# Layer 2 of a graph network: where the one-hot of each edge's target node is compared, turned and scaled

## The reference, cut to what matters

```python
proj = feat @ fc_weight.T
el, er = proj[src], proj[dst]                       # one row per edge
e = sum(leaky_relu(el + er, 0.2) * a, axis=-1)
gate = sigmoid(sum(el * er, axis=-1))
w = sigmoid(e * gate)                               # one weight per edge
neigh_sum = segment_sum(feat[src] * w[:, None], dst)
out = layernorm(x + (1 + eps) * feat + neigh_sum / max(deg, 1))
```

## Time and profile before

| what | value |
|---|---|
| median of 3 runs (lowest to highest) | 4249.38 us (4241.9 to 4252.88) |
| the profiled execution, first to last instruction (span) | 4202.4 us |
| median of the runs less that span | 47.0 us |
| layer 2's loop, first and last er+el (L1529) | 1644.2 to 4153.9 us |
| GpSimd's gathers L1449, 1624 of them | 1543.0 us, 950 ns each |
| VectorE's weigh L1461, 1632 | 477.5 us, 359 ns each |
| ScalarE's two comparisons L1556 and L1559, 406 each | 714 and 722 ns each |
| ScalarE's weight L1564, 407 | 202 ns each |

### The profile page before, as it was taken

One profiled execution on the slowest core, in us unless ns is written; L12 is line 12 of the kernel. 1 busy time (PEld: TensorE's weight loads), 2 busy tenths in 40 slices (PEclk: granted clock), 3 DMA queues, 4 the chain that ended last, 5 costly groups with the idle time before them and its releaser, 6 DMA issues. The chain is left out here.

```text
span 4202.4 us, 64915 instructions
## 1 busy us (share of the span) xinstructions
PE 2278.9 (54%) x13842; PEld 1815.0 (43%) x13842; DVE 2546.9 (61%) x12793; ACT 1628.2 (39%) x3531; POOL 2103.2 (50%) x2223
## 2 busy tenths in 40 slices
PE   1757575756667783445544444454444444444444
PEld 1535353544445443444443443444444444444443
DVE  6535353534444275667666676666676767667667
ACT  2424242433333244444443443443444444434344
POOL 3252434343343203666656565666656666656652
PEclk9878787878878896666666666656666666656666
DMA  7121111111111215444444444444444445444443
GB/s 145 32 54 31 51 34 48 38 44 42 41 48 34 58 49 169 138 132 136 134 133 129 123 137 128 130 137 128 136 125 131 134 132 139 129 135 129 128 129 96
DMA packets 357885, 425.07 MB, mean 101 GB/s; under 512 B 174163, under 2 KB 242141, under 8 KB 357740
## 3 DMA queue, kind: packets, MB, share of 16 engines
q0 software_dynamic: 103728, 266.13, 22.4%
q1 hardware_dynamic: 251800, 156.64, 14.5%
q10 hardware_dynamic: 2212, 0.60, 0.1%
HBM read 399.44 MB, written 23.70 MB: 101 GB/s over the span
## 5 line engine op out<-in xcount | busy, mean ns | idle before, releaser
L1449 POOL DMA_INDIRECT got<-rows,idx x1624 | 1543.0, 950 | 1038.3 <-issue 487.4
L1618 PE MATMUL sum_ps<-whot,got 128*128 128x128 f32 x3264 | 762.0, 410 | 1146.7 <-remote 416.6
L1618 PEld LDWEIGHTS sum_ps<-whot,got 128*128 128x128 f32 x3264 | 660.8, 301 | 1236.9 <-remote 433.6
L763 POOL DMA_INDIRECT got<-x_rows,idx x532 | 516.5, 971 | 789.5 <-DMA idx<-src_rows 630.7
L918 ACT CAST work<-c_ps 128x318 bf16<-128x318 f32 x1092 | 451.3, 431 | 845.0 <-remote 439.6
L945 PE MATMUL span_ps<-x_parts,work 128*126 128x393 bf16 x2756 | 667.9, 353 | 20.0 <-issue 20.0
L1611 PE MATMUL er_ps<-win,hot_t 128*128 128x128 bf16 x4932 | 525.4, 284 | 204.4 <-issue 121.0
L994 PE MATMUL c_ps<-right,left 128*128 128x318 bf16 x1092 | 338.0, 317 | 467.9 <-issue 281.2
L1611 PEld LDWEIGHTS er_ps<-win,hot_t 128*128 128x128 bf16 x4932 | 476.9, 134 | 234.7 <-issue 131.6
L1461 DVE TENSOR_SCALAR whot<-iota_f,dl,w_s 128x128 f32<-128x128 f32 x1632 | 477.5, 359 | 124.1 <-issue 121.7
L1517 DVE CUSTOM_DVE_ANT_0 small_rows<-got,er_ps 128x128 f32<-128x128 f32 x1624 | 387.3, 281 | 154.6 <-issue 116.3
(11 more groups left out here) (240 smaller groups left out, 2101.7 us busy)
## 6 DMA issues: line engine op xcount, KB each, us to landing
work<-dst_row SPq DMA_DIRECT2D x413, 256.0 KB
got<-rows,idx POOLq DMA_INDIRECT x1624
win<-parts SPq DMA_DIRECT2D x118, 96.0 KB
got<-x_rows,idx POOLq DMA_INDIRECT x532
idx<-src_rows SPq DMA_DIRECT2D x413, 2.0 KB
parts<-split SPq DMA_DIRECT2D x13, 384.0 KB
x_rows<-x_parts SPq DMA_DIRECT2D x2, 2320.5 KB
rows<-nodes SPq DMA_DIRECT2D x13, 256.0 KB, 2.8
```

The source lines that it names most:

```text
L763: pool.indirect_dma_start(got[:, c, i, 0:3 * D], None, x_rows, bass.IndirectOffsetOnAxis(ap=idx[:, c, i:i + 1], axis=0)).then_inc(gathered ...
L1449: pool.indirect_dma_start(got[:, c, i, :], None, rows, bass.IndirectOffsetOnAxis(ap=idx1[:, c, i:i + 1], axis=0)).then_inc(gathered[c], 16)
L1618: mm = pe.matmul(sum_ps[:, 0:P], got[:, c, i, D:2 * D], whot[:, c, i, :], start=(c == 0 and i == 0), stop=(c == NS - 1 and i == STEP - 1))
```

## The change

The targets are stored as 16-bit integers (`dst_row`, `dst_b`). VectorE now makes `hot_t`, with one comparison for a chunk's 512 edges against the partition's node number (`node_no`), 5 chunks ahead. TensorE then turns `hot_t` back, with the identity as the second operand, into the chunk's own PSUM bank `er_ps`, once `larger` has read that bank for the last time. ScalarE copies it from there, scaled by the weights, into `whot`. The column-wise targets (`dl_in`, `first_dl`, `dl`) and their two DMAs per body go. TURN becomes 5 and EXPAND 4.

```diff
-EXPAND = 5
-TURN = 6
+EXPAND = 4
+TURN = 5
...
-    dst_row = nc.dram_tensor("dst_row", [1, NBT * P * P], F32).ap()
+    dst_row = nc.dram_tensor("dst_row", [1, NBT * P * P], I16).ap()
...
 SyncE
-                        sp.wait_ge(less_done, k + 1)
+                        sp.wait_ge(node_done, k + 1)
                         sp.sem_inc(body_begun, 1)
                         load_first(k + 1)
-                        col = column(sp, k)
-                        sp.wait_ge(dl_done, k + 1)
-                        sp.sem_inc(body_begun, 1)
-                        sp.dma_start(dl_in[:], dst_rows[:, bass.ds(col, GROUP)]).then_inc(body_in, 16)
-                        sp.dma_start(first_dl[:], first_row[:, bass.ds(k, 1)].to_broadcast([P, 1])).then_inc(body_in, 16)
...
-                            sp.wait_ge(apart_done, NS * k + c + 1)
+                            sp.wait_ge(hot_done, NS * k + c + 2)
...
 VectorE
-                    def weigh(c, n):
-                        dve.wait_ge(w_done, n + 3)
-                        for i in range(STEP):
-                            at = c * STEP + i
-                            m = dve.tensor_scalar(whot[:, c, i, :], iota_f[:], dl[:, at:at + 1], w_s[:, c, i:i + 1],
-                                                  ALU.is_equal, ALU.mult)
-                        m.then_inc(whot_done, 1)
+                    def match(c, k):
+                        m = NS * k + c
+                        dve.wait_ge(dst_in[c], 16 * k + 16)
+                        dve.wait_ge(node_done, k + 1)
+                        dve.wait_ge(turned_back, m - TURN + 1)
+                        dve.tensor_scalar(hot_t[:, c, :], dst_b[:, c, :], node_no[:], None, ALU.is_equal
+                                          ).then_inc(hot_done, 1)
+
+                    def number(k):
+                        dve.wait_ge(first_in, 16 * k + 16)
+                        dve.wait_ge(hot_done, NS * k + 1)
+                        dve.tensor_scalar(node_no[:], first_t[:], pos[:], None, ALU.add).then_inc(node_done, 1)
...
                             if c == LATE:
-                                dve.wait_ge(body_in, 48 * k + 48)
-                                dve.wait_ge(whot_done, n)
+                                dve.wait_ge(body_in, 16 * k + 16)
                                 dve.sem_inc(body_begun, 1)
                                 dve.reg_mov(now, dve.value_load(at_now[0:1, 0:1], min_val=0, max_val=N - 1))
-                                dve.tensor_scalar(dl[:], dl_in[:], first_dl[:], None, ALU.subtract
-                                                  ).then_inc(dl_done, 1)
+                                number(k + 1)
...
+                            match((c + TURN) % NS, k + (c + TURN) // NS)
                             score((c - 1) % NS, n - 1)
-                            if c == LATE:
-                                dve.wait_ge(dl_done, k + 2)
-                            dve.wait_ge(summed, n + 1)
-                            weigh((c - 2) % NS, n - 2)
                             gated((c - 1) % NS, n - 1)
...
 ScalarE
-                    def match(c, k):
...
-                        act.activation(apart1[:], dst_b[:, c, :], ACT.Abs, bias=less[:]).then_inc(apart_done, 1)
...
-                        act.activation(hot_t[:, c, :], apart1[:], ACT.Relu, scale=-1.0, bias=one1[:]
-                                       ).then_inc(hot_done, 1)
+                    def weigh(c, n):
+                        act.wait_ge(turned_back, n + 3)
+                        act.wait_ge(w_done, n + 2)
+                        act.wait_ge(summed, n + 2)
+                        for i in range(STEP):
+                            m = act.activation(whot[:, c, i, :], er_ps[:, c, i * P:(i + 1) * P], ACT.Copy,
+                                               scale=w_s[:, c, i:i + 1])
+                        m.then_inc(whot_done, 1)
...
-                            if c == 1:
-                                offset(k + 1)
-                            match((c + TURN) % NS, k + (c + TURN) // NS)
                             weight((c - 1) % NS, n - 1)
+                            weigh((c - 1) % NS, n - 1)
...
 TensorE
+                    def turn_back(c, n):
+                        pe.wait_ge(l_done, n + 3)
+                        for i in range(STEP):
+                            mm = pe.matmul(er_ps[:, c, i * P:(i + 1) * P], hot_t[:, c, i * P:(i + 1) * P], ident_b[:],
+                                           start=True, stop=True)
+                        mm.then_inc(turned_back, 1)
...
-                        pe.wait_ge(whot_done, n + 3)
+                        pe.wait_ge(whot_done, n + 4)
...
-                            pe.wait_ge(l_done, n + 1)
+                            pe.wait_ge(whot_done, n + 1)
                             expand((c + EXPAND) % NS, k + (c + EXPAND) // NS)
                             if c == LATE + 1:
                                 pe.wait_ge(added, k + 1)
                                 sum_rows(0, n - LATE - 1)
                             if c != LATE:
                                 sum_rows((c - LATE) % NS, n - LATE)
+                            turn_back((c - 1) % NS, n - 1)
```

More of the change, by code:

```diff
@@ L1353, in graph_layers @@
             win_in = [sem(f"win_in{h}") for h in range(2)]
[L1354 to L1355 removed]
+            node_done = sem("node_done")
+            turned_back = sem("turned_back")
             hot_done = sem("hot_done1")
@@ L1496, in _ @@
                     dve.memset(er_ps[:, NS - 1, :], 0.0).then_inc(zeros_set, 1)
[L1497 to L1498 removed]
+                    dve.memset(hot_t[:, NS - 1, :], 0.0).then_inc(zeros_set, 1)
+                    dve.tensor_tensor_reduce(pr_s[:, 0, :], ident[:], iota_f[:], 1.0, 0.0,
                                              ALU.mult, ALU.add, pos[:]).then_inc(zeros_set, 1)
[L1500 removed]
                     dve.wait_ge(zeros_set, 9)
[L1502 to L1503 removed]
+                    dve.sem_inc(hot_done, 1)
+                    number(0)
+                    for c in range(TURN):
+                        dve.wait_ge(dst_in[c], 16)
+                        dve.wait_ge(node_done, 1)
+                        dve.tensor_scalar(hot_t[:, c, :], dst_b[:, c, :], node_no[:], None, ALU.is_equal
+                                          ).then_inc(hot_done, 1)
                     dve.sem_inc(leaked, 1)
@@ L1542, in _ @@
                     score(NS - 1, last)
-                    weigh(NS - 2, last - 1)
                     gated(NS - 1, last)
-                    weigh(NS - 1, last)
                     add_body(dve.snap(before, min_val=0, max_val=N - 1), bodies)
@@ L1564, in weight @@
                         act.activation(w_s[:, c, :], eg_s[:, c, :], ACT.Sigmoid).then_inc(w_done, 1)
-                    def offset(k):
-                        act.wait_ge(first_in, 16 * k + 16)
-                        act.wait_ge(apart_done, NS * k)
-                        act.activation(less[:], first_t[:], ACT.Identity, scale=-1.0, bias=pos[:]).then_inc(less_done, 1)
-                    act.sem_inc(hot_done, 1)
-                    act.wait_ge(zeros_set, 9)
-                    act.wait_ge(first_in, 16)
-                    act.activation(less[:], first_t[:], ACT.Identity, scale=-1.0, bias=pos[:]).then_inc(less_done, 1)
-                    for c in range(TURN):
-                        act.wait_ge(dst_in[c], 16)
-                        act.wait_ge(less_done, 1)
-                        act.wait_ge(hot_done, c + 1)
-                        act.activation(apart1[:], dst_b[:, c, :], ACT.Abs, bias=less[:]).then_inc(apart_done, 1)
-                        act.wait_ge(apart_done, c + 1)
-                        act.activation(hot_t[:, c, :], apart1[:], ACT.Relu, scale=-1.0, bias=one1[:]
-                                       ).then_inc(hot_done, 1)
+                    def weigh(c, n):
[6 more added lines that the diff above has]
+                        m.then_inc(whot_done, 1)
+                    act.wait_ge(zeros_set, 9)
+                    act.sem_inc(whot_done, 2)
                     for q in range(NQ):
@@ L1623, in _ @@
                     pe.sem_inc(summed, NS - LATE)
+                    pe.sem_inc(turned_back, 1)
                     for c in range(EXPAND):
```

27 lines of the change are left out of this document (6 added, 21 removed).

## The result

| | before | after |
|---|---|---|
| median, runs of one chip | 4241.05 us (4224.44 to 4260.55) | 4262.32 us (4232.07 to 4272.06) |
| span of the profiled execution | 4202.4 us | 4243.5 us |

The ratio is 1.0035, 95% interval 1.0021 to 1.0048: slower by a third of a per cent, where 4.2% faster was forecast. The profiled executions lie 41 us apart and the medians 21, so one profile can't carry a difference of 0.3%; what it can show is why nothing of the 4.2% came.

The account below looks back on a forecast made before the run. The prediction took VectorE's pace, slowed by standstills during gathers, as the bound. Its only nonzero term, -179 us from VectorE's fewer instructions, took 4249.4 to 4070 us; own range 3980 to 4170, 8-in-10 range 3810 to 4270.

Parts of the forecast that it names:

- VectorE's work: Layer 2 loop: VectorE loses `weigh`, 1.02 us a step, and gains one 16-bit comparison, 0.30 us between starts.
- The undisturbed step of 3.25 us: VectorE's step without standstills: 3.97 - 1.02 + 0.30 = 3.25 us; in full worth 292 us over 406 steps.
- Four copies: ScalarE gains four 128-column copies out of PSUM, 0.3 us each, 1.2 us a step; covered by VectorE, nothing saved or lost.
- Four turns: TensorE gains four bf16 matmuls of 128 columns, 0.50 us a step, last in its step; cost 0, up to +0.1 us.
- New waits: `match` waits for `turned_back` of two chunks before, `expand` for ScalarE's copies; each has one step of slack, cost 0.
- I let the step scale with: VectorE's step follows its instruction count, 28.3 to 26.3: 6.22 to 5.78 us, 179 us less over 406 steps.
- The 5.0 us are the floor, and VectorE's pace is the bound.: GpSimd's four gathers a step, 1.25 us apart, take 5.0 us; the rest of 6.22 us is waiting for VectorE and TensorE.
- Nothing comes back: Rival, 15%: engines share an allowance of instructions in a run of gathers; added ones eat the gain, 4249 us.
- the wide range: The 8-in-10 range, 3810 to 4270 us, taking in rivals without a gain and most of the larger gain.
- More comes back: Rival, 13%: VectorE always catches up and GpSimd hardly pauses; 5.2 us a step, 414 us less, 3835 us.
- The hand-overs decide: Rival, 17%: buffer release through TensorE and ScalarE lengthens some 200 GpSimd pauses by 1.39 us: +278 less 179, 4348 us.
- The port: Rival, 5%: VectorE's comparison holds up GpSimd by its whole 0.30 us each step, 122 us, 4192 us.

Follow-up runs that it names:

- e4: The changed kernel with its four gathers by index a step replaced by plain transfers of fixed rows (wrong rows): 3202.8 us, 0.7584.
- e5: The kernel before with its four gathers by index a step replaced by plain transfers of fixed rows (wrong rows): 3330.4 us, 0.7906.
- e3: The kernel before with 16-bit targets and `match` on VectorE; `weigh` stays there and nothing is turned back: 4217.9 us, 0.9993.
- e1: The changed kernel with the turn back placed ahead of the sum in TensorE's step: 4188.0 us, 0.9918 of before.
- e6: The changed kernel with the turn ahead of the sum on TensorE, and EXPAND 3, TURN 4: 4169.4 us, 0.9903 of before.
- e8: The changed kernel without TensorE's turn; ScalarE copies whatever the bank holds, so sums are wrong: 4190.1 us, 0.993 of before.
- e2: The changed kernel with EXPAND 3 and TURN 4, one more step of slack for `match` and `expand`: 4190.9 us, 0.9937 of before.

## Why the prediction was wrong

- *VectorE's work.* The comparison's 0.38 us came out at 379 ns, 0.27 between starts (forecast 0.30). Right. The undisturbed step of 3.25 us was not reached: e4 runs at 3.71 against e5's 4.02, 0.31 us a step of the 0.72 counted.
- *ScalarE.* Four copies take 1.14 us, forecast 1.2, each 369 ns. Right.
- *TensorE.* Four turns 0.63 us at the lower and 0.39 at the higher clock, forecast 0.50. The size was right. Its place, behind the sum, was counted for `expand` alone; what waits for it too is ScalarE's copy, behind 2.08 us of sum. Putting it first gained 1.2% against after (0.9918 to 1.0035).
- *New waits, "cost 0, on that cover".* Wrong. The step of slack was measured in VectorE's undisturbed steps, and 192 of TensorE's 319 recorded updates of `turned_back` came over 1 us late, these by 5.7 us on average, more than such a step. VectorE's idle time in front of `match` is 1.9 us a step (730 us in 1700 to 4100 us, some 380 steps). It isn't all loss: the idle time that VectorE had within its products and `weigh` before (351 us put down to `issue` in those 2400 us) is down to 28. The wait took its place. The rows of before, then of after, 1700 to 4100 us:

```profile
DVE q_s L1517 <- issue: 128.4, 186, 1.8
DVE small_rows L1517 <- issue: 112.8, 177, 1.5
DVE whot L1461 <- issue: 109.7, 214, 1.3
```

```profile
DVE hot_t L1453 <- remote: 687.4, 182, 10.9
DVE small_rows L1517 <- issue: 25.0, 53, 0.5
DVE q_s L1517 <- issue: 3.0, 6, 1.0
```

- *The step that failed: "I let the step scale with" the count of instructions, 6.22 to 5.78 us.* With 158 instructions more in 1000 us (e3) the time was 0.9993. The standstills weren't a price per instruction: how much VectorE had to do didn't matter (e3), and whether the gathers went by index did (e4, e5). The form was read right in the earlier trace rows, the cause of the length was not.
- *"The 5.0 us are the floor, and VectorE's pace is the bound."* Wrong as well: no experiment on the engines alone came near 5.8 us. The distance of 1.25 us was read within a run; over the window it was 1000 / 643 = 1.55 us. I read the difference as waiting for VectorE. With less or other work on the engines (e1, e3, e6, e8) it stayed at 1.53 to 1.56.
- *The rivals.* "Nothing comes back" gave nearly the right number, 4249 us, by a mechanism that falls: e8 has 590 matmuls less in 1000 us than after and doesn't beat e1. That 4262 us lies inside the wide range, up to 4270, is luck: that end was there for this rival. "More comes back" falls, since GpSimd's waits went up from 1.34 to 1.41 us a step. "The hand-overs decide" had the right place and a price that the cycle mostly hides: e1 and e2 show about 1% for it, some 45 us and not 278, and it was set against 179 us that didn't exist. "The port" falls: gathers last 958 ns on average, against 950, and in after the 219 that overlap a comparison between 1700 and 4100 us last 968 ns against 956 for the others. The lock that the Trainium skill describes ("SBUF — State Buffer", "SBUF: two separate sides") shows no price of note here.

## What to carry to other kernels

Before the work of an engine is priced, ask at what rate the queue that feeds it can go over a hundred steps, not over eight: the best distance between two starts is no floor if no long window ever shows it. A cheap test is to replace the suspected transfers by plain ones, and to take work off the engine that seems to bound: if the first moves the time by a quarter and the second by 1% or less, the work isn't the bound. And slack for a new hand-over is to be counted against the longest late update in the trace, not against the undisturbed step.

## What the runs showed of the hardware

- Before and after, where gathers by index start 1.25 us apart in runs and 1.56 and 1.58 us apart on average, semaphore updates of TensorE arrive late, by 4.3 to 5.7 us on average (those over 1 us, up to 14 us), and VectorE's by 1.4 to 3.1; ScalarE's weren't in either. The rows land on time: in after the last data packet of a gather ended 2.4 us after the gather's start in the median, 3.7 us at the 99th percentile.
- A gather by index of 96 rows takes GpSimd 921 ns and one of 128 rows 950 to 962 in the versions with four a step; half the bytes change nothing (956 ns). A plain transfer of as many rows takes it 0.54 to 0.60 us, and with plain transfers alone (e4) no update in the loop was over 1 us late.
- 512 16-bit integers compared with one value per partition, written as bf16, cost VectorE 0.27 us between starts; a 128-column float32 copy out of PSUM with a scale per partition costs ScalarE 0.26.
